# Layer two's scan inside a block: one recurrence of second order in place of two coupled ones of first order

## The reference, cut to what matters

```python
steps = sigmoid(steps_raw);  G = relu(G_raw);  A = relu(A_raw)
S = 1 + steps * G
alpha = 1.99 * tanh(steps**2 * A / S / 1.99)
M = [1/S, -alpha/steps; steps/S, 1 - alpha]        # per channel, constant in time
F = [steps/S * Bu; steps**2/S * Bu]                # Bu = x @ B
(z, y)[t] = M @ (z, y)[t-1] + F[t]                 # scan over the 1024 positions
s = y @ C + x * D
```

## Time and profile before

| | us |
|---|---|
| median of three runs | 4453.52 |
| profiled execution | 4459.22 |
| its span | 4456.3 |
| PE busy in the span | 4138.4 (93%) |
| DVE busy | 2755.8 (62%) |
| ACT busy | 1931.6 (43%) |
| POOL busy | 1690.0 (38%) |

### The profile page before, as it was taken

One profiled execution on the slowest core, in us unless ns is written; L12 is line 12 of the kernel. 1 busy time (PEld: TensorE's weight loads), 2 busy tenths in 40 slices (PEclk: granted clock), 3 DMA queues, 4 the chain that ended last, 5 costly groups with the idle time before them and its releaser, 6 DMA issues. The chain is left out here.

```text
span 4456.3 us, 72817 instructions
## 1 busy us (share of the span) xinstructions
PE 4138.4 (93%) x28636; PEld 3280.3 (74%) x28636; DVE 2755.8 (62%) x5175; ACT 1931.6 (43%) x3576; POOL 1690.0 (38%) x1337
## 2 busy tenths in 40 slices
PE   8699999999999997999999999999995999999894
PEld 8556566566565564889888888989894777788774
DVE  6467777777777775443434344343433788888886
ACT  2134444444444443544444454444442444444441
POOL 2233333333333342443444344344432233433333
PEclk9999999999999998999999999999997999999998
DMA  9501111111110101232323233232224343444423
GB/s 313 162 25 35 34 34 34 34 35 34 39 34 30 39 30 64 56 61 41 67 44 64 39 70 59 44 66 46 41 34 127 96 101 79 112 110 96 112 56 43
DMA packets 254003, 294.21 MB, mean 66 GB/s; under 512 B 21600, under 2 KB 226656, under 8 KB 251616
## 3 DMA queue, kind: packets, MB, share of 16 engines
q0 software_dynamic: 88064, 117.74, 15.8%
q1 hardware_dynamic: 165600, 171.82, 12.0%
HBM read 155.15 MB, written 134.35 MB: 65 GB/s over the span
## 5 line engine op out<-in xcount | busy, mean ns | idle before, releaser
L564 DVE TENSOR_TENSOR e_hTl<-e_hf,e_hTh 128x512 fp32r<-128x512 f32 x512 | 354.6, 693 | 801.6 <-ACT e_hTh L506 762.5
L1077 POOL TENSOR_TENSOR a_mix<-a_tmp,a_h 128x512 f32<-128x512 f32 x320 | 389.4, 1237 | 797.7 <-PE ps L1376 745.5
L425 POOL DMA_INDIRECT acc_d<-e_y,e_sids x256 | 408.6, 1596 | 708.9 <-DVE e_y L580 656.1
L505 ACT ACTIVATE e_hf<-ps_heads,e_b 128x512 f32<-128x512 f32 x512 | 354.2, 692 | 679.7 <-PE ps_heads L663 621.3
L663 PE MATMUL ps<-e_w2h,e_hTh 128*128 128x256 f32 x2048 | 578.7, 283 | 0.0
L663 PE MATMUL ps<-e_w2h,e_hTl 128*128 128x256 f32 x2048 | 577.3, 282 | 0.3 <-issue 0.2
L663 PE MATMUL ps<-e_w2l,e_hTh 128*128 128x256 f32 x2048 | 571.6, 279 | 0.8 <-issue 0.6
L663 PE MATMUL ps_heads<-e_xTh,e_w1h 128*128 128x512 f32 x1024 | 418.7, 409 | 16.2 <-ACT e_hTh L506 10.3
L663 PE MATMUL ps_heads<-e_xTl,e_w1h 128*128 128x512 f32 x1024 | 405.6, 396 | 0.0
L663 PE MATMUL ps_heads<-e_xTh,e_w1l 128*128 128x512 f32 x1024 | 405.6, 396 | 0.0
L663 PEld LDWEIGHTS ps<-e_w2h,e_hTh 128*128 128x128 f32 x2048 | 385.7, 188 | 20.3
(11 more groups left out here) (293 smaller groups left out, 9390.8 us busy)
## 6 DMA issues: line engine op xcount, KB each, us to landing
r_x<-in_L_attn_hidden_states SPq DMA_DIRECT2D x32, 512.0 KB, 6.4
xn_d<-r_xn SPq DMA_DIRECT2D x32, 512.0 KB, 4.6
xnT_d<-r_xT SPq DMA_DIRECT2D x32, 512.0 KB, 3.9
acc_d<-a_zeros POOLq DMA_DIRECT2D x32, 512.0 KB, 3.0
s_d<-a_s SPq DMA_DIRECT2D x32, 512.0 KB, 2.8
e_w<-in_L_ffn_w SPq DMA_DIRECT2D x16, 1024.0 KB
f_a<-acc_d SPq DMA_DIRECT2D x32, 512.0 KB, 3.8
f_x<-s_d SPq DMA_DIRECT2D x32, 512.0 KB, 5.2
```

The costliest lines, as they stand in the source:

```text
L425: pool.indirect_dma_start(acc_d, bass.IndirectOffsetOnAxis(ap=sids[:, GT * q + t:GT * q + t + 1], axis=0), ys[r][:, t, :], None, compute_o ...
L505: nc.scalar.activation(hf[m % 2][:], ps[2 + m % 2][:], ACT.Gelu, bias=b1s[:, m:m + 1])
L564: nc.vector.tensor_tensor(hT[q % 2][1][:, m, :], hf[m % 2][:], hT[q % 2][0][:, m, :].bitcast(F32), ALU.subtract).then_inc(h_sb, 1)
L1077: nc.gpsimd.tensor_tensor(mix[n][:, m, :].rearrange("p (c t) -> p c t", c=GT), tmp[i % 2][:].rearrange("p (c t) -> p c t", c=GT), h[q % 2] ...
```

## The change

The new step eliminates `z`. With `y[n]` for position n inside a block, the two coupled lines give `y[n+1] = (m11 + m12 + 1) y[n] - m11 y[n-1] + drive[n+1]`, where the drive now carries another factor `step`, which ACT applies when it copies the drive product out of PSUM. Step s computes position s + 1 from positions s and s - 1; step 0 has no older position and is one operation. After the last step `z` (now scaled by `step`) is the difference of the last two positions. The scaled `z` also goes through the block-to-block steps, so the power loop's third operation has no factor. In-block operations per expert are 30 (1 + 2 x 14 + 1) for 47, steps 40 for 41; part q=0 has ten steps for eleven, and its last slot one for two. The coefficients take 12 counted operations for 11. POOL, PE and the DMAs are unchanged.

```diff
-        CARRY = 1 + (SBLK - 1)
+        CARRY = SBLK - 1
         FIX = CARRY + NSB
         STEPS = FIX + SBLK + 1
-        FIX_N = 2 + 3 * (SBLK - 1) + 4 * NSB
+        CARRY_N = 1 + 2 * (SBLK - 2) + 1
+        FIX_N = CARRY_N + 4 * NSB
...
-        SPREAD = {QB - 1: (2, 2, 2, 2, 1, 1), 0: (2, 2, 2, 2, 1, 2), 1: (2, 2, 2, 2, 1, 1), 2: (2, 2, 2, 2, 1, 1)}
+        SPREAD = {QB - 1: (2, 2, 2, 2, 1, 1), 0: (2, 2, 2, 2, 1, 1), 1: (2, 2, 2, 2, 1, 1), 2: (2, 2, 2, 2, 1, 1)}
...
-        m11, m12, step = (coef[:, n:n + 1] for n in range(3))
+        m11, m12, near, drive_scale, far = (coef[:, n:n + 1] for n in range(5))
+        COEFS = 12
...
-            o.link(nc.vector.tensor_copy(coef[:, 2:3], st))
...
-            o.link(nc.vector.reciprocal(coef[:, 0:1], gd))
-            o.link(nc.vector.tensor_tensor(coef[:, 3:4], st, coef[:, 0:1], ALU.mult))
-            o.link(nc.vector.tensor_tensor(al, st, coef[:, 3:4], ALU.mult))
+            o.link(nc.vector.reciprocal(m11, gd))
+            o.link(nc.vector.tensor_scalar(far, m11, -1.0, None, ALU.mult))
+            o.link(nc.vector.tensor_tensor(al, st, m11, ALU.mult))
+            o.link(nc.vector.tensor_tensor(drive_scale, st, al, ALU.mult))
+            o.link(nc.vector.tensor_copy(al, drive_scale))
...
-            o.link(nc.vector.reciprocal(gd, st))
-            o.link(nc.vector.tensor_scalar(al, al, -1.99, None, ALU.mult))
-            o.link(nc.vector.tensor_tensor(coef[:, 1:2], al, gd, ALU.mult))
+            o.link(nc.vector.tensor_scalar(m12, al, -1.99, None, ALU.mult))
+            o.link(nc.vector.tensor_scalar(near, m12, 1.0, None, ALU.add))
+            o.link(nc.vector.tensor_tensor(near, near, m11, ALU.add))
...
-                    o.link(nc.vector.tensor_copy(z[:], ends[:, :, :, 0]))
-                    o.did(nc.vector.tensor_scalar(ends[:, :, :, 0], z[:], step, None, ALU.mult))
+                    o.did(stt(out=ends[:, :, :, 1], in0=ends[:, :, :, 0], scalar=near, in1=ends[:, :, :, 1],
+                              op0=ALU.mult, op1=ALU.add))
                 elif s < CARRY:
-                    o.n = 2 + 3 * (s - 1)
-                    was, now = ends[:, :, :, s - 1], ends[:, :, :, s]
+                    o.n = 1 + 2 * (s - 1)
+                    older, old, now = (ends[:, :, :, s + n] for n in (-1, 0, 1))
                     o.wait()
-                    o.link(stt(out=t[:], in0=was, scalar=m12, in1=now, op0=ALU.mult, op1=ALU.add))
-                    o.link(stt(out=z[:], in0=z[:], scalar=m11, in1=t[:], op0=ALU.mult, op1=ALU.add))
-                    o.did(stt(out=now, in0=z[:], scalar=step, in1=was, op0=ALU.mult, op1=ALU.add))
+                    o.link(stt(out=t[:], in0=old, scalar=near, in1=now, op0=ALU.mult, op1=ALU.add))
+                    o.did(stt(out=now, in0=older, scalar=far, in1=t[:], op0=ALU.mult, op1=ALU.add))
+                    if s == CARRY - 1:
+                        o.wait()
+                        o.did(nc.vector.tensor_tensor(z[:], now, old, ALU.subtract))
...
-                o.link(stt(out=qy[:, n + 1, :], in0=qz[:], scalar=step, in1=qy[:, n, :], op0=ALU.mult, op1=ALU.add))
+                o.link(nc.vector.tensor_tensor(qy[:, n + 1, :], qz[:], qy[:, n, :], ALU.add))
...
-                                     ACT.Copy, scale=coef[:, 3:4]).then_inc(drive_sb, 1)
+                                     ACT.Copy, scale=drive_scale).then_inc(drive_sb, 1)
```

More of the change, by code:

```diff
@@ L1577, in layer1_phase @@
         raw = sb("f_raw", [P, 4])
-        coef = sb("f_coef", [P, 4])
+        coef = sb("f_coef", [P, 5])
         xs = [sb(f"f_x{r}", [P, GT, D]) for r in range(RX)]
@@ L1824, in _ @@
             dve.wait_ge(sig, 1)
-            o.link(nc.vector.tensor_copy(coef[:, 2:3], st))
             o.link(nc.vector.tensor_tensor(gd, gd, st, ALU.mult))
             o.link(nc.vector.tensor_scalar(gd, gd, 1.0, None, ALU.add))
-            o.link(nc.vector.reciprocal(coef[:, 0:1], gd))
-            o.link(nc.vector.tensor_tensor(coef[:, 3:4], st, coef[:, 0:1], ALU.mult))
-            o.link(nc.vector.tensor_tensor(al, st, coef[:, 3:4], ALU.mult))
+            o.link(nc.vector.reciprocal(m11, gd))
[3 more added lines that the diff above has]
+            o.link(nc.vector.tensor_copy(al, drive_scale))
             nc.vector.tensor_tensor(al, al, ad, ALU.mult).then_inc(alpha_in, 1)
             dve.wait_ge(alpha_out, 1)
-            o.link(nc.vector.reciprocal(gd, st))
-            o.link(nc.vector.tensor_scalar(al, al, -1.99, None, ALU.mult))
-            o.link(nc.vector.tensor_tensor(coef[:, 1:2], al, gd, ALU.mult))
-            coefs = o.n
+            o.link(nc.vector.tensor_scalar(m12, al, -1.99, None, ALU.mult))
+            o.link(nc.vector.tensor_scalar(near, m12, 1.0, None, ALU.add))
+            o.link(nc.vector.tensor_tensor(near, near, m11, ALU.add))
+            assert o.n == COEFS
             def low(part, whole, high):
@@ L1903, in scan @@
                     dve.wait_ge(drive_sb, QB * j + QB)
-                    o.link(nc.vector.tensor_copy(z[:], ends[:, :, :, 0]))
-                    o.did(nc.vector.tensor_scalar(ends[:, :, :, 0], z[:], step, None, ALU.mult))
+                    o.did(stt(out=ends[:, :, :, 1], in0=ends[:, :, :, 0], scalar=near, in1=ends[:, :, :, 1],
+                              op0=ALU.mult, op1=ALU.add))
                 elif s < CARRY:
-                    o.n = 2 + 3 * (s - 1)
-                    was, now = ends[:, :, :, s - 1], ends[:, :, :, s]
+                    o.n = 1 + 2 * (s - 1)
+                    older, old, now = (ends[:, :, :, s + n] for n in (-1, 0, 1))
                     o.wait()
-                    o.link(stt(out=t[:], in0=was, scalar=m12, in1=now, op0=ALU.mult, op1=ALU.add))
-                    o.link(stt(out=z[:], in0=z[:], scalar=m11, in1=t[:], op0=ALU.mult, op1=ALU.add))
-                    o.did(stt(out=now, in0=z[:], scalar=step, in1=was, op0=ALU.mult, op1=ALU.add))
+                    o.link(stt(out=t[:], in0=old, scalar=near, in1=now, op0=ALU.mult, op1=ALU.add))
[3 more added lines that the diff above has]
+                        o.did(nc.vector.tensor_tensor(z[:], now, old, ALU.subtract))
                 elif s < FIX:
                     k = s - CARRY
-                    o.n = 2 + 3 * (SBLK - 1) + 4 * k
+                    o.n = CARRY_N + 4 * k
                     zk, yk = zc[r][:, :, k], yc[r][:, :, k]
@@ L1984, in _ @@
             o = Order(dve, power_o)
-            dve.wait_ge(coef_o, coefs)
+            dve.wait_ge(coef_o, COEFS)
             for n in range(SBLK):
@@ L2038, in drive @@
                 q, r = k % QB, k // QB
-                act.wait_ge(coef_o, 11)
+                act.wait_ge(coef_o, COEFS)
                 act.wait_ge(drive_ps, g + 1)
                 nc.scalar.activation(U[r][:, GT * q:GT * (q + 1), :], ps[0][:].rearrange("p (b t) -> p b t", b=GT),
-                                     ACT.Copy, scale=coef[:, 3:4]).then_inc(drive_sb, 1)
+                                     ACT.Copy, scale=drive_scale).then_inc(drive_sb, 1)
             def gate(g, m, begin):
```

## The result

The changed kernel takes 4403.35 us (median of four runs, 4401.49 to 4407.82), the kernel before 4455.12 (four runs, 4452.66 to 4464.64; three of them gave the 4453.52 above). The ratio is 0.9881, with a 95% interval of 0.9864 to 0.9898: 52 us less, 1.2%.

What follows compares the result with a forecast made beforehand. DVE's queue was taken to bound two tiles of four per expert, PE the others. Savings of 43.4 (tiles), 4.3 (end) and 1.0 (start) make 48.7 us off the 4453.5 median: 4404.8, stated as 4404, range 4391 to 4419.

Steps and rivals of the forecast that it cites:

- The bound: Per expert, DVE's queue binds tiles q=3 and q=0, which can give back at most 4.9 and 4.7 us; PE binds two.
- The price of the operation: In-block scan step on DVE: 1.24 us less 0.39 leaves a pair at 0.85; 0.96 where nothing stands between.
- The stalls: DVE operations beside POOL's products in q=3 and q=0: price unchanged; possible 0.2 to 0.4 us a tile, none taken.
- The rival of multiplied stalls: DVE, running earlier, stalls one more operation in each of 14 tiles: 13.6 us back, 4418; chance 0.12.
- rival (2): One more two-input DVE operation meets POOL's products in each of 14 tiles, 0.97 us each: 4418; chance 0.12.
- The end and the start: After the last drive 4.3 us saved; at the start, sixteen plain additions for scaled ones save 1.0 us.
- Rival (4): Shifted waits keep PE on its low clock longer after expert boundaries; 17 us longer per q=0 tile gives 4464; chance 0.02.
- The sum: Whole kernel: 43.4 us from seven q=3 and seven q=0 tiles, 4.3 end, 1.0 start: 48.7 us off.
- rival (3): Stalls partly vanish and a shorter `f_xn` wait removes a slow PE stretch: 5 to 15 us more, 4390 to 4399; chance 0.13.

Runs made afterwards that it cites:

- narrowed kernels: Kernel before and changed kernel, each with GpSimd's input-gate and output-gate products cut from 512 to 8 columns: 4382.15 us and 4354.99 us.
- early start: Changed kernel plus ninth `f_xd` buffer; q=0 skip products start once PE has transposed x, others when DVE has finished its turn: 4370.67 us, ratio 0.9842.

## Why the prediction was right, point by point

**The bound.** Right: two tiles of four were DVE's. The gain of q=3 and q=0 is in tiles where DVE, from its first product on, was idle for only 1.0 to 1.1 us in some 28 (I had called that back to back), and the narrowed kernels put PE's floor at 27.1 to 27.2 us, near the 27.4 that I had taken.

**The price of the operation.** Right: pair 0.86 us for the 0.85 taken, 0.96 at the end, where nothing stands between (0.96 taken). The operation on two strided columns and one contiguous has a median of 0.45 us, and `z` takes 0.40 with its gap where I took 0.5. Step 0 gained nothing, as said.

**The stalls.** The term that was mis-sized. I put 0.2 to 0.4 us a tile on them and took none; it was 1.1 in q=3 (4.6 a tile, from the second on, less the 3.5 of the count) and some 0.6 in q=0. The four stalls of q=3 were 1.41, 1.27, 1.25 and 1.33 us of duration and are 1.34, 0.81, 1.38 and 0.81. The direction was seen (a stall falling in part into a product that reads PSUM), but not the size; it happens at both pairs of q=3. With 9 x 0.39 = 3.5 this gives the 4.6 us that a q=3 tile lost, and putting the operations back brings it back. In q=0 only the first pair falls so, since the second still meets the small block-to-block operations, 1.29 and 1.22. The rival of multiplied stalls was wrong for these tiles; the Trainium skill's rule ("SBUF — State Buffer", section "Who interferes with whom") holds as far as runs here show: operations with two SBUF inputs are held, the product with one in PSUM is nearly not, 0.74 us for 0.69.

**What I had not seen.** The q=1 tiles became longer by 4.5 us in sum. I had said that they begin at the same scan step and are PE's; I hadn't followed POOL's queue, whose skip products wait for a transfer. That is rival (2) in another place: one or two operations held up, by 0.8 to 1.6 us in all, in four of the seven q=1 tiles, and one by 0.3 in a fifth.

**The end and the start.** The steps from the last split on took 8.0 us and take 5.2 (forecast 5.3):

```profile
4321.92 0.70 DVE L1881 TENSOR_TENSOR ps<-f_act,ps 128x512 f32<-128x512 f32 x1 [2.86 <-PE ps L2122]
...
4331.85 0.45 DVE L1913 SCALAR_TENSOR_TENSOR f_t<-f_U,f_coef 128x128 f32<-128x128 f32 x1
...
4337.03 0.25 DVE L1924 SCALAR_TENSOR_TENSOR f_t<-f_zc,f_qz,f_z 128x16 f32<-128x16 f32 x1
```

The wait of the fourth product for PE grew from 0.70 to 2.86 us: what DVE saved before it was lost, as expected. The plain addition takes 0.161 us, the 0.16 taken.

**The slow stretch of PE.** Rival (4) did not come: the wait for `f_w3l` is the same, and the mean granted clock over the seven q=0 tiles is 0.90 to 1.00 after and 0.87 to 0.95 before.

**The sum.** 48.7 forecast, 54.4 in layer two's profile, 51.8 between the medians. That 4404 and 4403.35 are so near is luck: the q=3 and q=0 tiles gave 11 us more than forecast, mostly stalls, which is the first half of rival (3); q=1 and q=2 took 5 back; and the two medians lie 5 us closer together than the two profiled spans (56.6, of which 2.1 ahead of layer two). The mechanism was right, the near hit of the sum was not earned.

## What to carry to other kernels

Where a queue runs nearly back to back beside an engine with a small lead, price a removed operation by its start-to-start time, and cap it by the distance of that tile to the other engine's own. Then follow the waits of every engine that shares something with the queue, here GpSimd's by way of an output transfer: once the q=0 tile was shorter, the transfer issued in it landed later in the next one, and its waiter met other work. GpSimd's products cost least here where VectorE had nothing to do; which wait starts them is worth as much attention as their length.

## What the runs showed that I had not expected

The lower of TensorE's two clock levels behind the expert boundary goes with the wait ahead of it, though not strictly. In the changed kernel the q=0 tiles behind a wait of 3.8 us have a first product 10 to 11 us after the drive, and a mean granted clock of 0.90 or 0.95 over the tile:

```profile
3863.94:3898.12 34.18, 29.42 (x156) 0.95 0.49 136
```

With a wait of 2.75 us it stands at 9.1 in most and at 7.5 in a few tiles (clock 1.00, above), and with the waits of 1.5 us and less of the early start at 6.2 to 6.5 in all. The length of the wait is not all of it: in the changed kernel with narrowed products two tiles behind waits of 3.5 and 3.3 us kept a granted clock of 1.00 (first product at 8.3 and 8.1), and others behind 3.4 us did not (0.90 and 0.95). What decides between them the runs don't show. A single VectorE operation took 2.71 us for 0.45 beside two GpSimd products in a row, where two operations in other places shared the same two.
